# Two routed expert stages: tiles fetched by register-addressed plain transfers, results scattered to token order, second matrices held on chip

## The reference

```python
# layer 0: 8 experts, the best 2 of each token, hidden width 512, exact GELU
topk_values, topk_indices = jax.lax.top_k(router_logits, TOP_K)
topk_weights = jax.nn.softmax(topk_values.astype(jnp.float32), axis=-1).astype(x.dtype)
h1 = jax.nn.gelu(jnp.einsum('bth,efh->btef', x, w1) + b1, approximate=False)
expert_outputs = jnp.einsum('btef,ehf->bteh', h1, w2) + b2
mixed_output = jnp.sum(topk_expert_outputs * topk_weights[..., None], axis=2)
# layer 1: 8 experts, the best 1 of each token, hidden width 256, ReLU
h = jax.nn.relu(jnp.einsum('td,edh->teh', tokens, W1) + b1[None])
y = jnp.einsum('teh,ehd->ted', h, W2) + b2[None]
out = jnp.take_along_axis(y, expert[:, None, None], axis=1)[:, 0, :]   # times max_prob
```

## Time and profile before

| | |
|---|---|
| median of 3 runs | 1636.05 us (1633.65 to 1636.2) |
| the profiled execution, its own time | 1640.13 us |
| its span in the trace | 1638.3 us |
| PE / DVE / ACT / POOL busy | 81% / 52% / 51% / 33% |
| mean granted clock of PE | 0.912 of full |

### The profile page before, as it was taken

The page is one execution under the profiler, slowest core; times in us unless marked ns, Lnnn a source line. Parts: engine busy times, 40 slices in busy tenths (PEclk is TensorE's granted clock), DMA queues, the critical chain, the costliest instruction groups (busy, mean ns, idle before and its releaser), DMA issues.

```text
span 1638.3 us, 22200 instructions
## 1 busy us (share of the span) xinstructions
PE 1328.1 (81%) x6934; PEld 743.1 (45%) x6934; DVE 854.0 (52%) x2721; ACT 831.8 (51%) x1885; POOL 546.9 (33%) x511
## 2 busy tenths in 40 slices
PE   5999999999999888876549658788889897796460
PEld 2434434444443345444248636455555554444250
DVE  3444543453344354674522176777666775557525
ACT  4777677677677535453225345446454552343130
POOL 3455455455445411323454342100000110112253
PEclk9999999999999989987769879889999997887685
DMA  9000000000000000000259600000000000000172
GB/s 371 23 1 1 1 1 1 1 1 1 1 1 1 1 0 1 1 1 13 85 187 339 222 26 9 6 1 1 1 1 1 1 1 0 1 1 7 37 234 59
DMA packets 35074, 67.30 MB, mean 41 GB/s; under 512 B 5424, under 2 KB 21296, under 8 KB 33808
## 3 DMA queue, kind: packets, MB, share of 16 engines
q1 hardware_dynamic: 29328, 54.37, 9.6%
q0 software_dynamic: 5056, 10.36, 2.1%
q10 hardware_dynamic: 576, 1.16, 0.2%
HBM read 47.71 MB, written 18.15 MB: 40 GB/s over the span
## 4 chain that ended last, share of the span: by engine, by line
PE 60%; DVE 19%; issue 8%; ACT 5%; DMA 5%; POOL 2%; DVEq 0%; ACTq 0%; POOLq 0%
PE bank L503 8%; PE bank L485 7%; PE bank L493 6%; PE bank L432 5%; DMA work<-xs,xi 4%; PE bank L608 3%; PE bank L806 3%; PE bank L475 3%; PE bank L565 3%; PE bank L579 3%; PE bank L802 2%; DVE work L1321 2%; PE bank L594 1%; PE bank L672 1%; POOL xs L1866 1%
## 5 line engine op out<-in xcount | busy, mean ns | idle before, releaser
L1813 POOL TENSOR_TENSOR work<-work 128x512 f32<-128x512 f32 x256 | 266.5, 1041 | 277.6 <-DVE work L1329 277.6
L944 ACT ACTIVATE work<-bank,work 128x512 f32<-128x512 f32 x256 | 176.5, 689 | 117.8 <-DVE work L1321 117.6
L1321 DVE TENSOR_REDUCE work<-bank 128x1 f32<-128x512 f32 x256 | 176.7, 690 | 76.7 <-PE bank L485 75.8
L493 PEld LDWEIGHTS bank<-cst,work 128*128 128x128 f32 x1024 | 110.5, 140 | 164.4 <-issue 106.0
L493 PE MATMUL bank<-cst,work 128*128 128x128 f32 x1024 | 160.0, 283 | 6.6 <-ACT work L952 6.1
L1329 DVE RECIPROCAL work<-work 128x1 f32<-128x1 f32 x256 | 41.9, 164 | 222.6 <-ACT work L944 222.3
L952 ACT ACTIVATE work<-bank 128x512 f32<-128x512 f32 x256 | 152.6, 596 | 0.5 <-PE bank L493 0.5
L1914 POOL TENSOR_TENSOR work<-work 128x512 f32<-128x512 f32 x32 | 40.9, 1277 | 332.4 <-PE bank L806 312.6
L485 PE MATMUL bank<-work 64*128 64x512 f32 x512 | 144.5, 641 | 3.4 <-ACT work L944 3.4
L1853 POOL TENSOR_TENSOR work<-work 128x1232 f32<-128x1232 f32 (+1 forms) x32 | 55.5, 1735 | 250.3 <-DVE work L1401 250.2
L503 PE MATMUL bank<-work 128*64 128x512 f32 x512 | 137.4, 617 | 0.7 <-ACT work L952 0.7
(11 more groups left out here) (232 smaller groups left out, 2550.0 us busy)
## 6 DMA issues: line engine op xcount, KB each, us to landing
W<-in_wC SPq DMA_DIRECT2D x39, 578.0 KB
xs<-gat SPq DMA_DIRECT2D x9, 1024.0 KB, 16.5
W<-in_wF SPq DMA_DIRECT2D x23, 321.0 KB
ys<-work SPq DMA_DIRECT2D x62, 64.0 KB
x_all<-in_x SPq DMA_DIRECT2D x4, 256.0 KB, 8.7
W<-in_L_attn_Wq SPq DMA_DIRECT2D x2, 512.0 KB, 5.5
W<-in_L_attn_Wv SPq DMA_DIRECT2D x2, 512.0 KB, 7.6
W<-in_L_attn_Wo SPq DMA_DIRECT2D x2, 512.0 KB, 9.0
```

The costliest lines, as they stand in the source:

```text
L493: m = nc.tensor.transpose(out[:, k * P:(k + 1) * P], pA[u % 5][:, k * P:(k + 1) * P], ident)
L944: A(pA[u % 5], bank[u % 3][:, :], ACT.Exp, bias=nmax[:, u % 8:u % 8 + 1], accum_out=rsum[0][:, u % 8:u % 8 + 1]).then_inc(sem("a_e"), 1)
L1321: V.tensor_reduce(nmax[:, u % 8:u % 8 + 1], bank[u % 3][:, :], AX, ALU.max, negate=True)\
L1813: G.tensor_tensor(pA[u % 5], pA[u % 5], rsum[1][:, u % 8:u % 8 + 1].to_broadcast([P, S]), ALU.mult)\
```

## The change

SP now fetches, per tile, two things with plain transfers whose addresses come from registers: the 128 token rows (they lie together in the sorted buffer) and the first matrix with both biases of the expert (330 KB in C, 198 KB in F), into rings of 6 (`NX`). For this it reads two numbers per tile, the expert `em` and the row block `xr`. The second matrices of all experts (2 MB for C, 1 MB for F) are loaded once and stay on chip, and PE reads the expert's number itself to address them. Each row of the sorted buffer is two words wider (`XW` = 130): the first chosen expert and the row of the result to which it goes. From these DVE makes, per tile, 128 indices (`idM`), and POOL scatters the tile's result with one indirect transfer to `yt`, in token order (a ring of 5, `NY`). Results are then read back by SP with plain transfers (`moe_back`: two per batch in C, one in F), and `moe_gather` is gone. C and F have a sorted buffer each; its filling is spread over phase A. SP starts the tile fetches only when all rows have been scattered; before, the weights didn't wait for that.

```diff
             def moe_turn(m_, j):
-                pe.wait_ge(sem(f"M_x{J % 3}"), 16 * (J // 3 + 1))
+                pe.wait_ge(sem(f"M_x{J % NX}"), 32 * (J // NX + 1))
             def moe_h(m_, j):
-                pe.wait_ge(sem(f"M_w{J % NW}"), 16 * (J // NW + 1))
+                chosen[J] = pe.value_load(em[0:1, j:j + 1], min_val=0, max_val=E - 1)
...
             def moe_y(m_, j):
-                    m = mm(out[:, 0:D], hTM[J % 3][:, f * P:(f + 1) * P], wM[J % NW][:, (ft + f) * P:(ft + f + 1) * P],
+                    m = mm(out[:, 0:D], hTM[J % 3][:, f * P:(f + 1) * P], second(m_)[:, bass.ds(chosen[J], 1), f * P:(f + 1) * P],
...
-            def moe_weights(m_):
+            def moe_tiles(m_, ph):
-                sp.wait_ge(sem("M_map"), m_["b0"] // NB + 1)
+                sp.wait_ge(sem(m_["free"]), NB * NT)
+                sp.wait_ge(sem("M_xi"), m_["b0"] // NB + 1)
+                sp.wait_ge(sem("M_sc"), 16 * NB * NT * (2 + m_["b0"] // NB))
                 for j in range(m_["tiles"]):
                     J = m_["j0"] + j
                     e = sp.value_load(em[0:1, j:j + 1], min_val=0, max_val=E - 1)
-                    if j >= NW:
-                        moe_put(J - NW)
-                    sp.dma_start(wM[J % NW][:, 0:m_["wide"]], T[m_["w"]][:, bass.ds(e, 1), :])\
-                        .then_inc(sem(f"M_w{J % NW}"), 16)
+                    r = sp.value_load(xr[0:1, j:j + 1], min_val=0, max_val=XS_ROWS // P - 1)
+                    if J >= NX:
+                        sp.wait_ge(sem("M_y"), J - NX + 1)
+                    sp.dma_start(xgM[J % NX], rows_of[:, bass.ds(r, 1), :]).then_inc(sem(f"M_x{J % NX}"), 16)
+                    sp.dma_start(slot(m_, J), T[f"w{ph}"][:, bass.ds(e, 1), :])\
+                        .then_inc(sem(f"M_x{J % NX}"), 16)
+            def moe_back(m_):
+                for i in range(NY):
+                    sp.wait_ge(sem(f"M_ys{i}"), 16 * len(range(i, m_["j0"] + m_["tiles"], NY)))
+                for b in range(NB):
+                    if b >= 4 // k:
+                        sp.wait_ge(sem("M_cb"), m_["b0"] + b - 1)
+                    for i in range(k):
+                        sp.dma_start(gat[...], back[b][:, :, i, :]).then_inc(sem(f"M_g{b}"), 16)
...
                 for j in range(m_["tiles"]):          # POOL
-                    G.indirect_dma_start(xgM[J % 3], None, T["xs"], bass.IndirectOffsetOnAxis(xi[:, j:j + 1], 0))\
-                        .then_inc(sem(f"M_x{J % 3}"), 16)
-                for b in range(2 if ph == 2 else NB):
-                    moe_gather(m_, b)
+                    pool.wait_ge(sem("M_y"), J + 1)
+                    G.indirect_dma_start(T["yt"], bass.IndirectOffsetOnAxis(idM[J % NY], 0), yM[J % NY], None)\
+                        .then_inc(sem(f"M_ys{J % NY}"), 16)
```

More of the change, by code:

```diff
@@ L54 @@
 XS_ROWS = (E - 1) * CAP + TILES0 * P
-NW = 7
-WIDE = FT0 * 2 * P + FT0 + P
-WIDE1 = FT1 * 2 * P + FT1 + P
+XW = D + 2
+NX = 6
+NY = 5
 PW = H * C + P - C + 1
@@ L299, in loaded @@
             eng.wait_ge(dma_in[what], 16 * n)
-        DMA_COUNT = {"x": 3, "small": 2, "late": 2, "A": 3, "B": 5, "D": 5, "E": 4, "zero": 10}
+        BLANKS = -(-(XS_ROWS // P) // 16)
+        DMA_COUNT = {"x": 3, "small": 2, "late": 2, "A": 3, "B": 5, "D": 5, "E": 4, "zero": 2 * BLANKS, "wC": 1, "wF": 1}
         ENDS = {0: [("a_pv", 32), ("a_o", 32)],
                 1: [("B_s", 16)],
-                2: [(f"M_ys{i}", 16 * len(range(i, TILES0, 3))) for i in range(3)],
+                2: [(f"M_ys{i}", 16 * len(range(i, TILES0, NY))) for i in range(NY)],
                 3: [("y_ready", 11), ("d_og", 32)],
@@ L332, in gathered, with slot, second @@
             return gat[:, i * D:(i + 1) * D]
+        def slot(m_, J):
+            n = m_["ft"] * P + m_["ft"] + D
+            at = m_["w1"] + (J % NX) * n
+            return W0[:, at:at + n]
+        def second(m_):
+            return v3(W0[:, m_["w2"]:m_["w2"] + E * m_["ft"] * P], E)
         owner = {}
@@ L671, in moe_h @@
                 for f in range(m_["ft"]):
-                    m = mm(out[:, f * P:(f + 1) * P], wM[J % NW][:, f * P:(f + 1) * P], xTM[J % 2], start=True, stop=True)
+                    m = mm(out[:, f * P:(f + 1) * P], slot(m_, J)[:, f * P:(f + 1) * P], xTM[J % 2], start=True, stop=True)
                 m.then_inc(sem("M_hp"), 1)
@@ L1535, in moe_map @@
                                             op0=ALU.mult, op1=ALU.subtract))
[L1536 to L1541, removed]
-                link(V.tensor_reduce(s2f[:, 0:every], own, AX, ALU.add))
-                link(V.scalar_tensor_tensor(out=s2f[:, 0:every], in0=s2f[:, 0:every], scalar=float(P), in1=rk[:, 0:every],
-                                            op0=ALU.mult, op1=ALU.add))
-                V.tensor_scalar(s2[:, 0:every], s2f[:, 0:every], -1.0, None, ALU.add).then_inc(sem("M_gi"), 1)
+                V.tensor_tensor(xr[:, 0:n], row[:, 0:n], const("tile")[:, 0:n], ALU.add).then_inc(sem("M_xi"), 1)
             def moe(ph):
@@ L1806, in link, with blank @@
                 pool.wait_ge(pool_chain, chain[0])
-            G.memset(gat[:, :], 0.0).then_inc(sem("zeroed"), 1)
+            link(G.memset(gat[:, :], 0.0))
+            loaded(pool, "small", DMA_COUNT["small"])
+            def blank(i):
+                G.tensor_scalar(v3(gat[:, 0:16 * XW], 16)[:, :, D + 1], const("slot")[:, 0:16],
+                                float(2 * NB * S + 2048 * i), None, ALU.add).then_inc(sem("zeroed"), 1)
+            blank(0)
             G.memset(run[:, 0:E], 0.0).then_inc(sem("zeroed"), 1)
             for u in range(NB * UNITS):
+                if u % 16 == 15 and u // 16 + 1 < BLANKS:
+                    loaded(pool, "zero", 2 * (u // 16 + 1))
+                    blank(u // 16 + 1)
                 pool.wait_ge(sem("a_r"), u + 1)
```

123 lines of the change are left out of this document (60 added, 63 removed).

## The result

The changed kernel takes 1656.26 us (median of 4 runs, 1654.18 to 1659.32), the one before on the same chip 1636.12: ratio 1.012, 95% interval 1.0089 to 1.015. The profiled execution took 1656.24 us, its span is 1654.4.

What follows compares the result with a forecast made beforehand. PE was taken as near the bound in C, SP's instruction issuing as F's; SP would then be slower than either present step. +22 + 16 - 7.7 - 3.5 - 1 - 2 + 0.6 = +24.4 us: 1660 us, range 1634 to 1676.

Steps and rivals of the forecast that it cites:

- the sum of +24.4: Whole kernel: all terms added, in us, giving 1664.5 against the profiled execution's 1640.1, or 1660 on the median.
- SP 2.24 to 2.30 us a tile, taken as 2.27: Both tile loops: two reads and two addressed issues per tile on SP, slower than either loop's present step.
- The term for F: F's tile loop: 22 steps at 2.27 us, 49.9 in place of 34.7, +15.2; with the end +0.8, together +16.
- PE's read in series: C's tile loop: PE's read per tile counted in series, 0.60 us less some 0.1; step 2.6 us, C +22.
- The address instructions have only a product's length in front of them, and I count half: C's tile loop: PE's four address instructions per tile, 0.09 us each, half counted in the 2.6 us step.
- The pages: Skill pages: `tensor_load` floor about 600 ns, F's term some +30 if so; rival of hidden PE register work, 1645, chance 0.2.
- The ends: From last result to mixing, without gathers: C 13.7 us to 6, -7.7; F 8.7 us to 5.2, -3.5.
- The closings: The four closings after F, some of each beside POOL's gathers: -1 us (0 to -3).
- D with what follows: Stage D: 16 gathers leave POOL, -2 us (0 to -5); copies and index instructions, +0.6.
- They should be free at this pace: Both loops: SP's waits for the result six tiles back cost nothing; 6.8 us cover landing (some 2.5), products and bias.
- the prediction's rival of cheaper reads: Both loops: SP's reads and issues overlap, tile about 1.5 us; with PE's work hidden, sum -22, 1614 us; chance 0.14.
- The clock in F: Rival: F's clock falls; at half clock PE's step is 2.8 us in place of 2.27, +12, 1672; chance 0.08.

Runs made afterwards that it cites:

- h_pe: Changed kernel with PE reading the expert numbers of all tiles in groups of eight ahead of each tile loop: 1649.0 us, ratio 1.0054.
- e5_gather: Changed kernel with only its read-back undone, POOL gathering the results by indirect transfers again: 1670.2 us, ratio 1.0183.
- e3_both: Changed kernel with no read on PE (always expert 0's second matrix) and one read per tile on SP: 1633.9 us, ratio 0.9998.
- n_hoist: Changed kernel with SP's and PE's reads in groups of eight ahead of the tile loops, without runtime bounds checks: 1631.8 us, ratio 0.998.
- n_all: Changed kernel with the runtime bounds check of its three reads per tile left out: 1642.4 us, ratio 1.0046.
- h_sp: Changed kernel with SP reading all row blocks in groups of eight ahead of the loop, expert as row block over 16: 1656.3 us, ratio 1.0106.

## Why the prediction was right, and where it was not

- **Slower, through issuing and reading, not through transfers or products**: right. 1656.3 against 1660; the transfers' share even fell. That the time is within 4 us is in part luck: added up by stretches of the two traces, the sum of +24.4 is 8.3 too high, and half of that doesn't show in the medians, because the trace of before was 4.1 over its median.
- **SP 2.24 to 2.30 us a tile, taken as 2.27**: 2.17 measured for a tile without a long record, 2.27 as a mean over F. The term for F was +16 and is +16.4: the step is right (2.265), the tail behind the last turn is +1.3 in place of +0.8.
- **PE's read in series, "less some 0.1"**: right on average, 0.46 us a step in C, but not as a fixed price: it goes from nothing to the whole read with the landing of the weights. It shows directly in the gap between turn and first product, and `h_pe` removes the gap.
- **"The address instructions have only a product's length in front of them, and I count half"**: this step failed. They run under the eight queued matmuls of the first product, and cost nothing (steps of 1.90 us have all four in them). Against a step of 1.90, PE's is 0.49 longer from turn to second product (the read) and 0.10 longer from there to the next turn (late turns): 2.49 on average from 851 to 936 (2.475 over the whole loop), in place of 2.6. With the tail, +0.7 in place of +2, that is 6 of the 8 us by which the sum of +24.4 is too high.
- **The pages**: the Trainium skill, Advanced Engine Details and Errata, Sequencer Loop, says that engine instructions can be read and queued while a control instruction executes. In the trace what stands ahead of the read, the turn and the products before it, runs on during the read. The first product, which stands behind the read in the list, started only after the read's last instruction in all 62 tiles, in most of them 0.16 to 0.17 us after it, so the read was not hidden from it in that way. The Trainium skill, DMA: Bandwidth & Descriptors, Latency and other measured facts, gives a floor of about 600 ns for a `tensor_load`. The single loads here lie under it, at 270 to 372 ns at the median; loads of eight numbers took 520 to 1082.
- **The ends**: C -6.8 for -7.7, F -2.0 for -3.5. POOL's scatters are 1.26 us apart, the last results of a loop come faster, and so the last scatter of C starts 0.9 us after its result. That delay was left out. The closings gave -2.6 for -1, of which `e5_gather` loses 1.6 again, so this much comes from the gathers' absence. D with what follows gave -3.3 for -1.4; that stretch scatters by 5 us, so its size is open.
- **"They should be free at this pace: ... there are three more steps, 6.8 us"**: this step failed too, though it cost little here. From the bias that frees a slot to the turn that needs it are two steps, not three: 4.95 us at the changed kernel's pace, of which 4.45 are used, and the weights land some 3.25 us after their issue in C, not 2.5. The slack was half a microsecond on average, and in single tiles there was none: SP waited for results 13 times in C, and PE for weights four times (2.0 us). It is why `e3_both` gained only 22 us and not the 34 expected, and the prediction's rival of cheaper reads (1614) could not have come true with this ring: with reads nearly gone, `n_hoist` reached 1632.
- **The clock in F**: it was granted lower, 0.80 from about the first turn to the last in place of 0.93. The price was put too high: from 1597 to 1603 the clock was 0.51, and the turns from 1595.94 on are 2.59, 2.32 and 2.27 us apart, where the rival had put 2.8. Over F the step stayed at SP's pace.

Open: why the late turns in C are late where no wait for a landing is recorded, why the executions of `n_all` lie up to 9 us apart, and what makes the stretch between C and F differ by 5 us among kernels with nearly the same instructions in it.

## What to carry to other kernels

When a loop is made to address its own transfers, add up the instruction list of the issuing engine per turn of the loop (reads, checks, addresses, issues): it is a bound like any engine's busy time, and no busy share shows it. Read such numbers in groups ahead of the loop, under work that is waited for anyway, without the runtime check where the range is certain by construction. Then count the ring in steps from the event that frees a slot to the instruction that needs it, and give each part of a slot a semaphore of its own, waited for where that part is used: here, with the reads already out of the loops, that one step was worth 14 us. And don't expect the whole price of an instruction back when it goes: PE's read cost 0.46 us a step and its removal gave 0.15, because the ring stood just behind it.

## What was unexpected in the hardware

- The check behind a read costs nearly as much as the read: `n_all`, with two checks fewer per tile, brings SP's tile in F from 2.18 to 1.66 us at the median, 0.26 for each. 39 values on SP took 15 us with checks (828.8 to 843.8 in `h_sp`) and 3.6 us without (827.1 to 830.7 in `n_hoist`).
- One load of eight numbers takes 0.5 to 1.1 us, two to four times one of a single number, so about 0.09 us a number (39 in 3.6 us) in place of 0.3.
- PE's four address instructions (46 ns each) are free under eight queued matmuls, while its read delays the first product by anything from nothing to some 0.75 us: it starts when the turn ahead of it has its weights, and is hidden only where these land 0.7 us before PE is free (868.3 for the turn at 869.06).
